# Last stage of a two-layer kernel: u of a batch in four transfers onto four row groups, four buffers for o and the result

## The reference

```python
    # layer 0, last lines: its result x is, per pixel, a 17-long vector u times a 17 x 128 matrix of the batch
    msum = vsum + jnp.einsum('bnm,bmc->bcn', Qn, mat)
    out = gamma * (msum * tailor[:, None, :]).reshape(B, C, H, W)
    # layer 1, last lines: o is the result of the scan
    x = _mamba(x, W_in, conv_w, conv_b, W_x, W_dt, b_dt, A_log, D, W_out)
    x = jnp.transpose(x.reshape(B_, H, W, C), (0, 3, 1, 2))
    x = jax.nn.silu(_group_norm(x, gn_gamma, gn_beta))
    return x + x_hsi
```

## Time and profile before

| | us |
|---|---|
| median of 3 runs | 16720.4 |
| lowest, highest | 16718.77, 16725.19 |
| the profiled execution, its own time | 16713.74 |
| its span, first to last instruction | 16712.0 |
| phase_c in it, from its first load to the end | 16032.8 to 16712.0 |

### The profile page before, as it was taken

The page is one execution under the profiler, slowest core; times in us unless marked ns, Lnnn a source line. Parts: engine busy times, 40 slices in busy tenths (PEclk is TensorE's granted clock), DMA queues, the critical chain, the costliest instruction groups (busy, mean ns, idle before and its releaser), DMA issues. The chain is left out here.

```text
span 16712.0 us, 141790 instructions
## 1 busy us (share of the span) xinstructions
PE 14237.2 (85%) x40250; PEld 5369.3 (32%) x40250; DVE 14036.9 (84%) x13540; ACT 9963.5 (60%) x13655; POOL 13059.7 (78%) x5647
## 2 busy tenths in 40 slices
PE   8999988888888888888888888888888888888876
PEld 3333333333333333333333333333333333333322
DVE  1222229999999999999999999999999999999942
ACT  2222226666666666666666666666666666666631
POOL 0000009999999999999999999999999999999930
PEclk9999988999999999999999999999999999999965
DMA  1111104444444444444444444444444444444455
GB/s 49 42 44 38 39 27 167 166 169 169 166 169 169 169 166 166 166 167 162 167 168 169 169 166 169 169 166 169 167 167 162 166 167 167 169 169 167 168 194 211
DMA packets 508713, 2504.88 MB, mean 150 GB/s; under 512 B 53097, under 2 KB 164938, under 8 KB 226651
## 3 DMA queue, kind: packets, MB, share of 16 engines
q1 hardware_dynamic: 489723, 2419.71, 40.0%
q10 hardware_dynamic: 18208, 76.11, 1.2%
HBM read 2325.05 MB, written 170.57 MB: 149 GB/s over the span
## 5 line engine op out<-in xcount | busy, mean ns | idle before, releaser
L728 POOL TENSOR_TENSOR hc<-h,c_all 128x1024 f32<-128x1024 f32 x4096 | 9523.5, 2357 | 458.0 <-DVE h L1043 441.6
L940 PE MATMUL y_ps<-hc,ident 128*128 128x512 f32 x16392 | 8513.9, 665 | 1436.1 <-POOL hc L728 1434.1
L824 ACT ACTIVATE d_a<-dt,a_neg 128x512 f32<-128x512 f32 x8194 | 5594.9, 689 | 4215.2 <-DVE h L1043 4205.6
L1043 DVE TENSOR_TENSOR_SCAN h<-d_a,h,dbx_v 128x512 f32<-128x512 f32 x5456 | 6623.6, 1262 | 8.8
L940 PEld LDWEIGHTS y_ps<-hc,ident 128*128 128x128 f32 x16392 | 3304.4, 211 | 6533.9 <-issue 3802.1
L1030 DVE TENSOR_TENSOR dbx_v<-dtx_ps,b_all 128x1024 f32<-128x1024 f32 x2816 | 3316.3, 1208 | 60.3 <-DMA b_all<-bc_dram 24.4
L1043 DVE TENSOR_TENSOR_SCAN h<-d_a,h,dbx_p 128x512 f32<-128x512 f32 x2480 | 3024.4, 1261 | 0.0
L717 POOL TENSOR_TENSOR dbx_p<-dtx,b_all 128x1024 f32<-128x1024 f32 x1280 | 3000.2, 2353 | 25.0 <-DVE h L1043 2.0
L479 POOL MEMSET ident_f<- 128x128 f32 x1 | 0.2, 204 | 2416.7 <-POOLq L44 2416.7
L272 PE MATMUL conv_ps<-image,w_taps 128*32 128x512 f32 x11520 | 1778.8, 595 | 0.0
L362 DVE RECIPROCAL k_inv<-k_nrm 128x4 f32<-128x4 f32 x256 | 45.5, 178 | 1776.0 <-ACT k_nrm L214 1776.0
(11 more groups left out here) (123 smaller groups left out, 8958.7 us busy)
## 6 DMA issues: line engine op xcount, KB each, us to landing
b_all<-bc_dram SPq DMA_DIRECT2D x1028, 1024.0 KB, 6.3
c_all<-bc_dram SPq DMA_DIRECT2D x1025, 1024.0 KB, 4.8
o_dram<-o_sb SPq DMA_DIRECT2D x257, 256.0 KB, 5.6
o_t<-o_dram SPq DMA_DIRECT2D x64, 1024.0 KB, 11.0
out<-r_t ACTq DMA_DIRECT2D x64, 1024.0 KB, 9.2
image<-in_x SPq DMA_DIRECT2D x91, 512.0 KB, 4.0
un<-un_dram SPq DMA_DIRECT2D x516, 34.0 KB
bc_dram<-low_bc SPq DMA_DIRECT2D x257, 64.0 KB, 4.7
```

What stands on the lines that cost most here:

```text
L728: nc.gpsimd.tensor_tensor(hc[:, n % HC], h[:, n], c_all[:, n // CG % 2, n % CG].unsqueeze(1).broadcast_to([128, 2, CH]), ALU.mult).then_in ...
L824: nc.scalar.activation(d_a[:, half], dt[:, p, half], ACT.Exp, scale=a_neg[:, half, n:n + 1]).then_inc(a_done, 1)
L940: last = nc.tensor.matmul(y_ps[:, half], ident[:], hc[:, n % HC, half], start=False, stop=(n == S - 1))
L1043: nc.vector.tensor_tensor_scan(h[:, n, half], d_a[:, half], dbx, zero_col[:] if first else h[:, n, half, CH - 1:CH], ALU.mult, ALU.add).th ...
```

## The change

Only phase_c changes.

- `u_t` becomes 128 x 2 x 8 x 512. A batch of u is loaded at once, by four transfers: transfer g takes of every block its pixels 512g to 512g+511 and puts them on partitions 32g to 32g+16. A transfer is 17 x 8 x 512 with pieces of 2 KB in DRAM. There are two such buffers, so batch p+1 is loaded while batch p is in work. The matrices gm are loaded four times too, onto the same four groups of partitions.
- Matmul g of a block reads gm and u from partitions 32g to 32g+16, another group of TensorE's rows for each g, and writes bank g as before. The copies `ab` and `gm_b` are gone; ScalarE and TensorE read scale, shift and gm in place.
- o and the result have four buffers (CBUF). SP issues o of block k when silu of block k-4 is done.
- ScalarE issues the store of block k-2 ahead of silu of block k, after its wait for o of block k.
- SP issues u of batch p+1 behind the first o of batch p, and before that waits until the matmuls of batch p-1 are done.

```diff
-        gm = sb("gm_c", [KU, B, C])
-        gm_b = sb("gm_b", [KU, 2, C])
-        o_t = sb("o_t", [C, 2, CB])
-        u_t = sb("u_c", [KU, 2, CB])
+        gm = sb("gm_c", [128, B, C])
+        o_t = sb("o_t", [C, CBUF, CB])
+        u_t = sb("u_c", [128, 2, NCB, CH])
         act_t = sb("act_t", [C, 2, CB])
-        r_t = sb("r_t", [C, 2, CB])
+        r_t = sb("r_t", [C, CBUF, CB])
...
+            for g in range(groups):
+                sp.dma_start(gm[32 * g:32 * g + KU], gmat_dram.rearrange("b k c -> k b c")).then_inc(small_in, 16)
+            def load_u(i):
+                b, j0 = parts[i]
+                if i >= 2:
+                    sp.wait_ge(res_mm, first_of[i - 1])
+                c0 = (b * SLOTS + 1) * CH
+                for g in range(groups):
+                    sp.dma_start(u_t[32 * g:32 * g + KU, i % 2, j0:],
+                                 un_dram[:, c0:c0 + N].rearrange("k (j g n) -> k j g n", g=groups, n=CH)[:, j0:, g]
+                                 ).then_inc(u_in[i % 2], 16)
+
+            load_u(0)
+            for b, j, k in blocks:
+                s = k % CBUF
+                if k >= CBUF:
+                    sp.wait_ge(silu_done, k - CBUF + 1)
+                c0 = (b * NCH + 1) * CH + j * CB
+                sp.dma_start(o_t[:, s], o_dram[:, c0:c0 + CB]).then_inc(o_in[s], 16)
+                if k == first_of[part_of[k]] and part_of[k] + 1 < len(parts):
+                    load_u(part_of[k] + 1)
...
+            for b, j, k in blocks:
+                act.wait_ge(o_in[k % CBUF], 16 * (k // CBUF + 1))
+                if k >= 2:
+                    store(*blocks[k - 2])
+                nc.scalar.activation(act_t[:, k % 2], o_t[:, k % CBUF], ACT.Silu, bias=shift[:, b:b + 1],
+                                     scale=scale[:, b:b + 1]).then_inc(silu_done, 1)
...
+            for b, j, k in blocks:
+                pe.wait_ge(u_in[part_of[k] % 2], 16 * groups * (part_of[k] // 2 + 1))
+                if k >= 2:
+                    pe.wait_ge(added, k - 1)
+                for g in range(groups):
+                    last = nc.tensor.matmul(res_ps[:, k % 2, CH * g:CH * g + CH], gm[32 * g:32 * g + KU, b],
+                                            u_t[32 * g:32 * g + KU, part_of[k] % 2, j], start=True, stop=True)
+                last.then_inc(res_mm, 1)
...
-                dve.wait_ge(silu_done, b * NCB + 2)
-                dve.wait_ge(res_mm, b * NCB + 2)
-                nc.vector.tensor_copy(ab[:, 0, 0:1], scale[:, bass.ds(b, 1)]).then_inc(ab_done, 1)
-                nc.vector.tensor_copy(ab[:, 1, 0:1], shift[:, bass.ds(b, 1)]).then_inc(ab_done, 1)
-                nc.vector.tensor_copy(gm_b[:, 0], gm[:, bass.ds(b, 1), :].rearrange("k o c -> k (o c)")
...
+            for b, j, k in blocks:
+                dve.wait_ge(silu_done, k + 1)
+                dve.wait_ge(res_mm, k + 1)
+                if k >= CBUF:
+                    dve.wait_ge(stored[k % CBUF], 16 * (k // CBUF))
+                nc.vector.tensor_tensor(r_t[:, k % CBUF], act_t[:, k % 2], res_ps[:, k % 2], ALU.add).then_inc(added, 1)
```

More of the change, by code:

```diff
@@ L1156, in phase_c @@
         rooted = sem("C_rooted")
[L1157 to L1160, removed]
+        o_in = [sem(f"C_o_in{s}") for s in range(CBUF)]
+        u_in = [sem(f"C_u_in{s}") for s in range(2)]
         silu_done = sem("C_silu_done")
@@ L1163, in phase_c @@
         added = sem("C_added")
-        stored = [sem(f"C_stored{p}") for p in range(2)]
+        stored = [sem(f"C_stored{s}") for s in range(CBUF)]
         block = ctx.enter_context(nc.Block())
+        parts = [(b, 0) for b in range(B)]
+        blocks = [(b, j) for b, j0 in parts for j in range(j0, NCB)]
+        blocks = [(b, j, k) for k, (b, j) in enumerate(blocks)]
+        first_of = [sum(NCB - j0 for _, j0 in parts[:i]) for i in range(len(parts) + 1)]
+        part_of = [i for i, (_, j0) in enumerate(parts) for _ in range(j0, NCB)]
+        groups = CB // CH
         @block.sync
@@ L1185, in _, with store @@
+            for b, j, k in blocks:
[6 more added lines that the diff above has]
+                    load_u(part_of[k] + 1)
         @block.scalar
         def _(act):
+            def store(b, j, k):
+                act.wait_ge(added, k + 1)
+                act.dma_start(out[b, :, j * CB:j * CB + CB], r_t[:, k % CBUF]).then_inc(stored[k % CBUF], 16)
@@ L1187, in _ @@
             act.wait_ge(step, STEPS_BEFORE_ROOT)
             nc.scalar.activation(g_std[:], g_m2[:], ACT.Sqrt, bias=eps[:]).then_inc(rooted, 1)
[L1189 to L1200, removed]
@@ L1201, in _ @@
-            for p in range(2):
-                act.wait_ge(stored[p], 16 * (B * NCB // 2 + 1))
+            act.wait_ge(step, STEPS_BEFORE_USE)
+            for b, j, k in blocks:
[4 more added lines that the diff above has]
+                                     scale=scale[:, b:b + 1]).then_inc(silu_done, 1)
@@ L1204, in _ @@
+            store(*blocks[-2])
+            store(*blocks[-1])
+            for s in range(CBUF):
+                act.wait_ge(stored[s], 16 * len([k for _, _, k in blocks if k % CBUF == s]))
         @block.tensor
@@ L1209, in _ @@
             pe.wait_ge(step, STEPS_BEFORE_ROOT)
[L1210 to L1220, removed]
+            pe.wait_ge(small_in, 16 * (1 + groups))
+            for b, j, k in blocks:
[6 more added lines that the diff above has]
+                last.then_inc(res_mm, 1)
         @block.vector
@@ L1245, in _ @@
             dve.wait_ge(rooted, 1)
-            dve.wait_ge(small_in, 32)
+            dve.wait_ge(small_in, 16 * (1 + groups))
             chain(nc.vector.reciprocal(m2[:], g_std[:]))
@@ L1250, in _ @@
             chain(nc.vector.tensor_scalar(shift[:], m2[:], -1.0, gn[:, 1:2], ALU.mult, ALU.add))
-            dve.sem_inc(added, 2)
-            for b in range(0, B):
-                dve.wait_ge(silu_done, b * NCB + 2)
-                dve.wait_ge(res_mm, b * NCB + 2)
-                nc.vector.tensor_copy(ab[:, 0, 0:1], scale[:, bass.ds(b, 1)]).then_inc(ab_done, 1)
-                nc.vector.tensor_copy(ab[:, 1, 0:1], shift[:, bass.ds(b, 1)]).then_inc(ab_done, 1)
-                nc.vector.tensor_copy(gm_b[:, 0], gm[:, bass.ds(b, 1), :].rearrange("k o c -> k (o c)")
[L1259 to L1266, removed]
+            assert done[0] == STEPS_BEFORE_USE
+            for b, j, k in blocks:
[4 more added lines that the diff above has]
+                nc.vector.tensor_tensor(r_t[:, k % CBUF], act_t[:, k % 2], res_ps[:, k % 2], ALU.add).then_inc(added, 1)
 STEPS_BEFORE_SHARE = 1 + C // GROUP + 1 + 2
 STEPS_BEFORE_ROOT = STEPS_BEFORE_SHARE + 3
+STEPS_BEFORE_USE = STEPS_BEFORE_ROOT + 4
 def build(nc, t, out):
```

16 lines of the change are left out of this document (1 added, 15 removed).

## The result

The changed kernel took 16766.2 us (median of 10 runs, 16760.7 to 16773.0), the kernel before beside it 16723.1 us: a ratio of 1.0026 with a 95% interval of 1.0017 to 1.0035. It is 43 us slower. That lies inside the range of the prediction, 16710 to 16785, but 32 us above its likeliest time and 14 above the end of the forecast's own range, 16752. It is also just above the 0.2% (33 us) up to which the prediction spoke of no change. The profiled execution took 16762.1 us, its span 16760.1.

The account below looks back on a forecast made before the run. One DMA engine, 98% busy, was taken to bound phase_c before and after. Its work rises from 664 to 681 us: 17 loss - 6 at start and end + 3 hiccups = 14 more, 16734 us; range 16710 to 16785.

Parts of the forecast that it names:

- forecast's own range: Whole kernel, one engine bound before and after: 16715 to 16752 us, chance 0.68.
- The second rival: Phase_c's matmuls: row groups do not overlap, a block stays at 7.16 us; 54 us slower, 16774 us; chance 0.08.
- the third rival: Phase_c around u's stall: engine runs dry, o and result at 350 GB/s, 6.0 us a block, 16798 us; chance 0.18.
- fixed 13.50 us: Phase_c before: from u's issue to block k+1's matmuls always 13.50 us, taken as u's transfer setting the pace.
- Row groups: Phase_c's matmuls on four row groups: a block about 2 us instead of 7.16, off the bound, gaining no time by itself.
- gm: Start of phase_c: four gm loads instead of one, 13.1 us instead of 3.3, the added 9.8 us all on the path.
- Hand-over: Phase_c, from o and results to the next u: u issued at 28 us, engine busy to 36, no gap.
- The price of u's packets: Phase_c's u loads: 0.080 us per 2 KB packet, 43.5 us a batch against 42.5 before, loss 8 us in all.
- The walk of the prediction: One batch followed from the end of u: o and stores share the engine, 5.0 us a block, no gap before next u.
- The sign against the packet price: In phase_c's profile after: the packet price is wrong if a batch's 544 packets of u need more than 46 us.
- The sign against the one engine: In phase_c's profile after: the one-engine step is wrong if u's stretch shows over 30 GB/s for longer than a slice.
- Four buffers: Phase_c's o and result: removes waits but no packets; at most 14 us, the engine's idle 2%, taken as nothing.

Follow-up runs that it names:

- b_16rows: Kernel before, with u of a block loaded as rows 0 to 15 and row 16 instead of one transfer of 17 rows: 16530.7 us, ratio 0.9881.
- a_mm2: Changed kernel with each block's four matmuls issued twice over the same results: 16762.8 us, ratio 1.0025 to the kernel before.
- a_gm16: Changed kernel with gm's four transfers split into rows 0 to 15 and row 16: 16758.7 us, ratio 1.0020 to the kernel before.
- b_2k: Kernel before, with u of a block in four transfers of 17 x 512, packets of 2 KB instead of 8 KB: 16746.0 us, ratio 1.0010.
- a_gate: Changed kernel where SP waits until the next batch's u has landed before issuing a batch's second o: 16741.2 us, ratio 1.0013 to the kernel before.
- b_c4: Kernel before, with four buffers for o and the result instead of two, o issued earlier: 16760.0 us, ratio 1.0023.
- b_r4: Kernel before, with four buffers for o and the result, but o issued as late as before: 16722.7 us, ratio 0.9998.
- a_spread: Changed kernel with the next batch's four u transfers issued behind the first, third, fifth and seventh o: 16805.0 us, ratio 1.0046 to the kernel before.
- a_16rows: Changed kernel with u and gm each split into rows 0 to 15 and row 16: 16429.1 us, ratio 0.9821 to the kernel before.

## Why the prediction held, point by point

**What held, and what was luck.** The mechanism held: one DMA engine bounds the kernel before and after, so the change gains nothing. The time lies in the range partly by luck. The forecast by itself ended at 16752; the range went on to 16785 only for the rivals 2 and 3, and neither of them came. The 43 us came from something that was no term and no rival. And by the prediction's own 33 us the change is "slower", to which it gave 0.27, and not "same", to which it gave 0.66.

**What bounds the kernel: right.** The step from the fixed 13.50 us by the slow slices to one busy DMA engine was confirmed by b_16rows, which takes most of u off that engine, with one more transfer a block as the only other edit, and gains 198 us. It carried the forecast that neither row groups nor buffers would gain anything. The prediction sets a formula beside the 13.5 us: the Trainium skill's page "DMA: Bandwidth & Descriptors", section "Anatomy of one DMA", gives 2.0 us + bytes/436 GB/s. The section is about transfers that GpSimd issues, and u is issued by SP; and the 13.5 us also hold packets of the result, which take turns with u's on its engine. So the comparison does not test the page.

**Row groups: right.** Eight matmuls take 2.09 us; about 2 were taken from the column groups of the earlier trace rows:

```profile
16182.14 2.09 PE L1227 MATMUL res_ps<-u_c,gm_c 17*128 17x512 f32 x8 [2.83 <-DVE r_t L1266]
```

The second rival, groups that don't overlap, fell by this row, and a_mm2 bears out that up to 3.8 us a block cost nothing.

**gm: right in sign, a little high.** 9.8 us were taken for the three more loads. By the records of single packets the four take 13.6 us from the first packet to the last, 13.1 were worked out, and the one before took 5.0 beside the first o, where 3.3 were taken; so 8.6 us more. a_gm16, in which the four still take 4.5, gave 7. The first u arrived for the matmuls 60.0 us after the stage's start (16098.2), 59.6 were worked out.

**Hand-over: right.** The last u is issued while o and results keep the engine busy; with o and results alone a block takes 4.9 us, 5.0 were taken:

```profile
16263.62 2.29 DVE L1266 TENSOR_TENSOR r_t<-act_t,res_ps 128x2048 f32<-128x2048 f32 x1 [2.65 <-ACT act_t L1208]
16268.50 2.29 DVE L1266 TENSOR_TENSOR r_t<-act_t,res_ps 128x2048 f32<-128x2048 f32 x1 [2.60 <-ACT act_t L1208]
```

No slice is without packets, and the third rival as it was told, 350 GB/s for o and results, did not come.

**The price of u's packets: the term that was mis-sized.** "A batch of u: 544 x 0.080 = 43.5 us." The lone price is right, and b_2k confirmed it to a hundredth. But the last 65 or so packets of a batch's u run beside the first o loads behind them and take 0.16. So a batch takes 88.6 us instead of the 43.5 + 40.0 = 83.5 worked out: the six from the second u load to the last make 31 us, and the first, likewise late, 6 (the second block's addition began 116.5 us into the stage, 110.6 were worked out). 37 us, and 40 by the count of the 488 slow packets, is more than the 28 that were missing (721.9 measured, 679.6 + 14 = 693.6 forecast); the other terms were some 9 us high in sum, and which of them was not taken apart. The walk of the prediction put o's sixteenth on the bound engine behind u, but not that SP, as soon as it can issue at all, starts the other fifteen sixteenths beside it. a_gate takes that apart from the rest: 21 us back, net of what its own wait costs.

A row of the trace before could have told: while gm was loaded beside the first o, from 16035.9 us on, 78 packets of 512 B took 2.8 us, 0.036 each instead of the 0.024 of the earlier trace rows:

```profile
DMA packets 188, 0.93 MB, mean 333 GB/s; under 512 B 1, under 2 KB 79, under 8 KB 79
```

**The signs that it named.** The sign against the packet price came true: 544 packets were to need no more than 46 us, and they took 54.6 to 55.2 from the first to the last in each of the last six batches. Of the 9 us and more, 5 to 6 are the slow packets; in a_gate, without them, it is still 49.6, since at the start u takes turns with the last stores: in the changed kernel only 14 of its packets get through from 16182 to 16187 us, beside 148 packets of stores on all engines. The sign against the one engine, over 30 GB/s for longer than a slice in the u stretch, is there by its letter (five slices of 342 to 396), and misleads: the bytes above u's are o's on the other engines. ScalarE's longest waits for o were to be eight of 40 us; they are one of 59.8 before the first block, one of 48.3 and six of 55 to 56. Each of the long ones spans nearly all of a batch's u, which is why they came out longer than 40.

**Four buffers "worth nothing": wrong by itself.** It was bounded by the engine's idle 2%, so from one side only. b_c4 shows 37 us of loss, and b_r4 that it is all in the earlier issue of o. A bound engine that is 98% busy can't be made much busier, but its packets can be made slower; that this is what happens in b_c4 is likely and not shown.

## What to carry to other kernels

Look at the DMA view in slices shorter than a transfer: a steady 26 to 32 GB/s is one engine working for all, and its packets, counted over every transfer that has a share on it, were here a bound that no buffer, prefetch or faster compute engine touched. Splitting 17 rows into 16 and 1 was worth 198 us before and 337 after the change, more than all the rest; with that done, all else in the change, which had brought a loss, brought 95 us more (478 to 383 us of stage); which part of the change brings them was not taken apart. And when a queue is the bound, issuing more beside it is not free: the changed kernel lost 21 us or more (a_gate) and the kernel before 37 us (b_c4) by loads that started earlier than they had to.

## What was not expected of the hardware

- In the changed kernel a packet of 2 KB takes 0.080 us when other engines are quiet and 0.16 us while they load from DRAM; for that time one other engine's 8 KB packets take 0.6 to 0.7 instead of 0.31 us. In a_spread one such partner alone is enough; in b_2k 641 of 644 packets beside o loads were not slow. What the two share was not found.
- Loads of 96 rows, 6 an engine, ran beside u at 261 GB/s in all, loads of 128 rows, 8 an engine, at 358.
- SP was held in the issue itself while the one engine still had the transfers ahead to move: 9 to 16 us for three of four transfers of 136 packets, against 0.24 for the first of the four and for one of 17 before. In a_16rows, with the rows spread, eight issues took 4.4 us together. What holds SP was not shown. The Trainium skill's page "DMA: Bandwidth & Descriptors", section "Issuing engines are not separate DMA queues", calls the time to issue "usually small relative to the DMA itself"; here it was as long as the transfer's 136 x 0.080 = 10.9 us.
